# One core, conditioned transformer and state-space layers: three kinds of PSUM evacuation moved from ACT to DVE

## What is computed

```
mod = silu(cond) @ Wada + bada;  shift, scale, gate for attention and for the MLP
x = x + gate_a * attention(norm(x) * (1 + scale_a) + shift_a)
x = x + gate_m * (gelu(xm @ W1 + b1) @ W2 + b2)
```

```
h = norm(x) * (1 + scale) + shift
for each direction:  xs, z = split(h @ in_w);  xs = silu(xs);  dt = softplus(...)
    u = dt * xs;  B, C = rows of xs @ xproj            # 512 channels, 64 states
    hst[t] = hst[t-1] * exp(dt * A) + u * B;  y[t] = sum over states of hst * C
    out = ((y + xs * D) * silu(z)) @ out_w             # g is the gated output
x = x + gate * (forward + backward);  x = x + gate * ((silu(h @ w1) * (h @ w2)) @ w3)
```

## Time and profile before

| what | us |
|---|---|
| three runs | 3542.23, 3541.03, 3540.88 |
| median | 3541.03 |
| the profiled execution | 3532.22 |
| its span, first to last instruction | 3530.3 |
| mean granted TensorE clock of the profile | 0.953 |

### The profile page before, as it was taken

The page is one execution under the profiler, slowest core; times in us unless marked ns, Lnnn a source line. Parts: engine busy times, 40 slices in busy tenths (PEclk is TensorE's granted clock), DMA queues, the critical chain, the costliest instruction groups (busy, mean ns, idle before and its releaser), DMA issues.

```text
span 3530.3 us, 70435 instructions
## 1 busy us (share of the span) xinstructions
PE 3064.4 (87%) x21944; PEld 2666.9 (76%) x21944; DVE 2872.2 (81%) x3122; ACT 3086.7 (87%) x6820; POOL 2941.0 (83%) x1551
## 2 busy tenths in 40 slices
PE   6878898898988999888998889889898899988776
PEld 4567787787877877787787778778777788877765
DVE  1249998799888998789888898889988898889885
ACT  1269999999899998899998999999998999999995
POOL 0049988899888998889888898889988899899995
PEclk9589999999999999999999999999999999999999
DMA  5011111111111111111111111111111111111211
GB/s 167 0 30 45 46 42 40 48 50 45 39 48 40 52 43 40 47 47 46 43 41 46 47 46 40 48 40 51 45 41 46 45 46 44 42 43 43 54 47 27
DMA packets 170750, 162.54 MB, mean 46 GB/s; under 512 B 25834, under 2 KB 165098, under 8 KB 170356
## 3 DMA queue, kind: packets, MB, share of 16 engines
q1 hardware_dynamic: 170356, 157.69, 16.3%
HBM read 154.44 MB, written 3.18 MB: 45 GB/s over the span
## 4 chain that ended last, share of the span: by engine, by line
PE 31%; POOL 23%; issue 20%; ACT 16%; DVE 7%; SPq 1%; POOLq 0%; DMA 0%; ACTq 0%; DVEq 0%
POOL hst L395 18%; PE ps L1175 8%; PE ps L1191 7%; ACT dA L574 7%; POOL uBT L404 6%; PE ps L944 5%; ACT uBT L560 4%; DVE hst L864 3%; PE ps L953 2%; PE ps L1013 2%; PE ps L1064 1%; PE ps L991 1%; PE ps L1000 1%; PE ps L1074 1%; SPq L301 1%
## 5 line engine op out<-in xcount | busy, mean ns | idle before, releaser
L395 POOL TENSOR_TENSOR hst<-hst,C_sb 128x1024 f32<-128x1024 f32 x1024 | 2427.1, 2385 | 324.4 <-DVE hst L864 317.5
L864 DVE TENSOR_TENSOR_SCAN hst<-dA,ps 128x512 f32<-128x512 f32 x2048 | 2383.8, 1203 | 258.7 <-ACT dA L574 135.8
L574 ACT ACTIVATE dA<-dt,A 128x255 f32<-128x255 f32 x4096 | 1779.6, 500 | 102.1 <-DVE hst L864 96.8
L1175 PE MATMUL ps<-ident,uBT 128*128 128x128 f32 x8192 | 1275.3, 280 | 153.8 <-DVE hst L864 116.5
L1191 PE MATMUL ps<-ident,hst 128*128 128x128 f32 x8192 | 1273.2, 279 | 141.8 <-POOL hst L395 139.3
L1175 PEld LDWEIGHTS ps<-ident,uBT 128*128 128x128 f32 x8192 | 993.1, 145 | 286.3 <-DVE hst L864 151.0
L1191 PEld LDWEIGHTS ps<-ident,hst 128*128 128x128 f32 x8192 | 971.2, 143 | 204.0 <-POOL hst L395 203.1
L560 ACT ACTIVATE uBT<-uT,BT 128x512 f32<-128x512 f32 x1536 | 1045.6, 714 | 32.6 <-PE ps L1175 31.6
L404 POOL TENSOR_TENSOR uBT<-uT,BT 128x512 f32<-128x512 f32 x512 | 551.7, 1078 | 227.0 <-ACT uT L517 220.1
L475 ACT ACTIVATE probs<-ps,nmax 128x128 f32<-128x128 f32 (+1 forms) x256 | 104.8, 418 | 73.6 <-DVE nmax L735 73.6
L1013 PE MATMUL ps<-qk 32*128 32x256 f32 (+1 forms) x512 | 163.0, 400 | 0.6 <-DVE v L711 0.6
(11 more groups left out here) (141 smaller groups left out, 2138.3 us busy)
## 6 DMA issues: line engine op xcount, KB each, us to landing
C_sb<-c_dram SPq DMA_DIRECT2D x1024, 128.0 KB, 2.9
gate_l<-gate_rows_dram SPq DMA_DIRECT2D x16, 256.0 KB, 3.9
x_att<-in_x_dram SPq DMA_DIRECT2D x8, 256.0 KB, 3.6
w<-in_L_cond_W_dram SPq DMA_DIRECT2D x2, 1024.0 KB
out_dram<-x_glu SPq DMA_DIRECT2D x8, 256.0 KB, 3.2
hst<-in_L_cond_Wada_dram SPq DMA_DIRECT2D x1, 1536.0 KB
wg<-in_L_cond_mlp_w_dram SPq DMA_DIRECT2D x3, 512.0 KB
w_xp<-_L_cond_fwd_xproj_w_dram SPq DMA_DIRECT2D x1, 1280.0 KB
```

The costliest lines, as they stand in the source:

```text
L395: pool.tensor_tensor(h, h, C_sb[:, n % FED:n % FED + 1, :].to_broadcast([P, KI, NB]), ALU.mult).then_inc(hC_ready.sem, 1)
L574: done = act.activation(dA[:, n % NT, c, lo:hi], dt[:, d, c, lo:hi], ACT.Exp, scale=A[:, d, c, n:n + 1])
L864: dve.tensor_tensor_scan(pair(hst[:, n % NR]), pair(dA[:, n % NT]), ps[:, BANK_U + (2 * n + e) % (2 * NT), :][:, way], 0.0, ALU.mult, ALU. ...
L1175: last = pe.transpose(ps[:, BANK_U + (2 * n + e) % (2 * NT), o:o + P], uBT[:, n % NF, j, c * P:(c + 1) * P], ident[:, :])
```

## The change

Three steps change their engine, and their place among the steps does not. The `uT` copy and the `gT` copy become `tensor_copy` on DVE, of the same 128x1024 out of two PSUM banks. The scaled and shifted rows become `tensor_scalar` on DVE with the scale and shift columns as two per-partition operands, 128x256 twice for each norm. The waits for PE and the semaphores that tell of the results go with them. Each norm on DVE gets one more `sem_inc` on a counter that nobody waits for. Line numbers behind the edits shift: L864 is L865 in the new kernel, L804 is L798, L764 is L758, L782 is L776, L682 and L687 are L667 and L672.

```diff
--- before.py
+++ after.py
@@ -244,7 +244,7 @@
         pads_zero, pool_step, consts_ready, silu_ready, A_ready, mods_mm = map(
             sem, ("pads_zero", "pool_step", "consts_ready", "silu_ready", "A_ready", "mods_mm"))
         dve_setup, rows_ready, mods_ready, bn_turns = map(sem, ("dve_setup", "rows_ready", "mods_ready", "bn_turns"))
-        offset_turns, pool_turns = sem("offset_turns"), sem("pool_turns")
+        offset_turns, hT_turns = sem("offset_turns"), sem("hT_turns")
         gate0_in, gate1_in = flow("gate0_in", 16), flow("gate1_in", 16)
 
         norm_step = [flow(f"norm_step{s}", 2) for s in range(4)]
@@ -432,7 +432,7 @@
             act.wait_ge(mods_ready, 1)
             act.wait_ge(consts_ready, 7)
 
-            def norm(b, s, dst):
+            def norm(b, s):
                 for i in range(STEPS["norm"]):
                     if i == 2:
                         act.wait_ge(norm_step[s].sem, norm_step[s].at(b, 2))
@@ -452,13 +452,6 @@
                         for j in range(TT):
                             last = act.activation(xn[:, j, :], x_of[:, j, :], ACT.Identity, bias=offset[:, j:j + 1], scale=rstd[:, j:j + 1])
                         last.then_inc(xn_ready[s].sem, 1)
-                    if i == 5:
-                        act.wait_ge(xnT_mm[s].sem, xnT_mm[s].at(b, 1))
-                        for c in range(KD):
-                            col = bass.ds(b, 1)
-                            last = act.activation(dst[:, c, :], ps[:, BANK_P, c * NB:(c + 1) * NB], ACT.Identity,
-                                                  bias=mod_shift[:, s, c, col], scale=mod_scale[:, s, c, col])
-                        last.then_inc(hT_ready[s].sem, 1)
                     yield
 
             def heads(b, ti):
@@ -512,18 +505,10 @@
                     if i == 17:
                         act.wait_ge(one_ready.sem, one_ready.at(p, 1))
                         act.activation(dt[:, d], channels(uT[:, d]), ACT.Ln).then_inc(log_ready.sem, 1)
-                    if i == 22:
-                        act.wait_ge(uT_mm.sem, uT_mm.at(p, 1))
-                        act.activation(uT[:, d], ps[:, BANK_P:BANK_P + 2, :].rearrange("p a n -> p (a n)"), ACT.Copy).then_inc(uT_ready.sem, 1)
                     yield
 
             def post(p):
-                for i in range(STEPS["post"]):
-                    if i == 1:
-                        act.wait_ge(gT_mm.sem, gT_mm.at(p, 1))
-                        act.activation(gT[:, :, :].rearrange("p k n -> p (k n)"), ps[:, BANK_P:BANK_P + 2, :].rearrange("p a n -> p (a n)"),
-                                       ACT.Copy).then_inc(gT_ready.sem, 1)
-                    yield
+                yield from idle(STEPS["post"])
 
             def glu(b):
                 for i in range(STEPS["glu"]):
@@ -534,18 +519,18 @@
                     yield
 
             def layer0(b):
-                yield from norm(b, LN_ATT, hT)
+                yield from norm(b, LN_ATT)
                 yield from idle(STEPS["qkv"])
                 yield from heads(b, 0)
                 yield from heads(b, 1)
                 yield from idle(STEPS["proj"])
-                yield from norm(b, LN_MLP, hT)
+                yield from norm(b, LN_MLP)
                 yield from up(b)
                 yield from idle(STEPS["down"])
-                yield from norm(b, LN_SSM, hT_ssm)
+                yield from norm(b, LN_SSM)
 
             def close(b):
-                yield from norm(b, LN_GLU, hT)
+                yield from norm(b, LN_GLU)
                 yield from glu(b)
 
             def forcing(p, d, n):
@@ -686,6 +671,15 @@
                         for j in range(TT):
                             last = dve.bn_aggr(mv[:, j, :], stats[:, j, :])
                         last.then_inc(norm_step[s].sem, 1)
+                    if i == 5:
+                        dst = hT_ssm if s == LN_SSM else hT
+                        dve.wait_ge(xnT_mm[s].sem, xnT_mm[s].at(b, 1))
+                        dve.sem_inc(hT_turns)
+                        for c in range(KD):
+                            col = bass.ds(b, 1)
+                            last = dve.tensor_scalar(dst[:, c, :], ps[:, BANK_P, c * NB:(c + 1) * NB], mod_scale[:, s, c, col],
+                                                     mod_shift[:, s, c, col], ALU.mult, ALU.add)
+                        last.then_inc(hT_ready[s].sem, 1)
                     yield
 
             def residual(b, bank, rnd, gates, which, gate_in, mm, mul, done, x_old, x_new):
@@ -802,10 +796,17 @@
                         dve.wait_ge(dt_ready.sem, dt_ready.at(p, 1))
                         dve.wait_ge(in_ready.sem, in_ready.at(p, 1))
                         dve.tensor_tensor(pre, dt[:, d], xsT[:, :, :], ALU.mult).then_inc(u_ready.sem, 1)
+                    if i == 22:
+                        dve.wait_ge(uT_mm.sem, uT_mm.at(p, 1))
+                        dve.tensor_copy(uT[:, d], ps[:, BANK_P:BANK_P + 2, :].rearrange("p a n -> p (a n)")).then_inc(uT_ready.sem, 1)
                     yield
 
             def post(b, d):
                 for i in range(STEPS["post"]):
+                    if i == 1:
+                        dve.wait_ge(gT_mm.sem, gT_mm.at(2 * b + d, 1))
+                        dve.tensor_copy(gT[:, :, :].rearrange("p k n -> p (k n)"),
+                                        ps[:, BANK_P:BANK_P + 2, :].rearrange("p a n -> p (a n)")).then_inc(gT_ready.sem, 1)
                     if i == 8:
                         if d == 0:
                             dve.wait_ge(out_done.sem, out_done.at(b, 0))
```

## The result

Five timed runs of the changed kernel took 3517.93 to 3531.06 us, median **3522.52 us**, beside 3541.03 for the kernel before: ratio 0.995, 95% interval 0.9935 to 0.9966. It is faster by 18.5 us, where 9.8 were forecast; the time lies inside the range, the forecast ratio of 0.9972 outside the interval. The profiled execution took 3522.32 us (span 3520.5), where the sum gave 3522.4 for it.

A forecast was written before the change was run, and what follows sets the result against it. No engine was the bound throughout; PE, POOL, ACT and DVE took turns. Seven times the per-block terms gave -10.5 us, plus 0.3 and 0.4 made -9.8, taking 3541.0 to 3531 us; the 8-in-10 range was 3511 to 3558.

The forecast's parts named there:

- the one loss: GLU norm and u in the forward pass, where DVE has no gap: +2.3 us, 7 times.
- Term 1: GLU norm and u in the forward pass: DVE's added work delays PE and the GLU copies, +2.3 us, 7 times.
- Term 2: MLP norm: PE's wait before its first product goes, so it starts earlier; -1.3 us, 7 times.
- a dear case: GLU norm and u, forward pass: PE's longer stand also lowers its granted clock, costing some 4 us.
- Term 3: Attention norm: the product that waited 1.29 us starts earlier; -1.1 us, 7 times.
- Term 4: Gated output in the forward pass: ACT's decays and SiLU table load come earlier; -1.1 us, 7 times.
- Term 5: State-space norm: part of PE's 0.64 us wait goes; -0.4 us, 7 times.
- Term 6: Places near nothing: backward gated output 0, backward u +0.1 7 times, first forward pass +0.3, prologue and tail 2 x 0.2.
- A: Rival, slower: DVE's full stretch is paid and the leads elsewhere are lost; +17.5 us, 3558 us, chance 0.21.
- B: Rival, no change: leads half lost, -14, GLU and u loss stays, +16; 3540 us, chance 0.28.
- C: Rival, faster by more: the GLU norm and u loss is covered, 0 there; sum -26, 3515 us, chance 0.08.
- D: Rival: DVE becomes the bound everywhere and all 73 us show; 3614 us, chance 0.02.

The follow-up runs named there:

- att_mlp_gf: Kernel before with the attention and MLP norms' rows and the forward pass's gated-output copy moved to DVE; median 3512.71 us beside 3539.91, ratio 0.9916.
- no_u_glu: Kernel before with the attention, MLP and state-space norms' rows and both gated-output copies moved to DVE; median 3514.54 us beside 3541.29, ratio 0.9924.
- glu_u: Kernel before with the GLU norm's rows and the copy of u moved to DVE; median 3540.90 us beside 3536.78, ratio 1.0010.
- g_only: Kernel before with only the gated-output copy moved to DVE, in both passes; median 3533.96 us beside 3541.29, ratio 0.9973.
- att_mlp_g: Kernel before with the attention and MLP norms' rows and the backward pass's gated-output copy moved to DVE; median 3531.66 us beside 3536.78, ratio 0.9976.
- u_only: Kernel before with only the copy of u moved to DVE, in both passes; median 3555.24 us beside 3541.29, ratio 1.0038.

## Why the prediction was right, and where it was not

- **The sign and the mechanism** were right: DVE's extra 73 us (70 us busy in the moved rows; DVE's total rose by 57) did not show as such, and neither did ACT's 68 us of relief (its total fell by 49). The places decide, with both signs, and the one loss was named.
- **Term 1, +2.3, measured +1.8.** The step that failed is "the load waits for the fourth copy". The load came behind ACT's decays; only the SiLU behind it waits for the copy. In the kernel before decays and copy ended at the same 1552.57, so its timeline could be read either way. The DVE side was late as forecast (+2.28 to the first copy), and 1.1 us came back because the load moved under the copies. Its first distance was forecast as 15.4 us from the product to the load; it measured 14.3. Then 0.55 us are lost again between load and residual, which I had not looked at. I had also treated the two moved pieces as one sum, which happens to be right only because they are moved together: apart they cost more.
- **Term 2, -1.3, measured -1.65 in the first pair of profiles and about -2.3 against the second.** The wait gave 1.1, not 1.3: the product starts 2.00 us behind the transposes, where 1.8 was taken. The rest is PE's clock, and with both signs: in blocks 0 and 5 the kernel before had its first product at full speed and the changed kernel at the low level, and nothing was won there. I had seen the low clock in the GLU stretch and named it as a dear case there, and had not asked the same of the MLP norm, where the 2.07 us of the product in the earlier trace rows stood before me.
- **Term 3, -1.1, measured -0.7.** From the transposes to the product PE won 0.8. DVE's first copies, which were to come 0.2 earlier behind the statistics, came 0.26 later, and 0.93 were won behind them.
- **Term 4, -1.1, measured -1.2.** Right, step by step: two scans, the copy, and the load 3.28 us behind the copy's start.
- **Term 5, -0.4, measured +0.2.** DVE stood 0.78 us before the pair, so it was free in time, and still PE's product starts 7.57 us behind the statistics, before 7.39; nothing was won, and att_mlp_gf without it is as fast. The step that failed is "here ACT had fewer decays queued ahead": it had none, ACT stood 0.36 us before it made the rows, so there was no queue to save.
- **Term 6** held: backward gated output 0, backward u 0 but for the clock (+0.1 was taken), first forward pass +0.3. The tail cost about 1 us more than the 0.4 allowed.
- **From the profile to the median.** "The forecast for the median is 3541.0 - 9.8" carried the 8.8 us, by which the median lay above the profiled execution, over to the changed kernel. There the profiled execution and the median agree to 0.2 us. The profiled execution of the kernel before was a lucky one: it had the low clock behind the MLP norm in 4 blocks, the second one in 6, which is 4.9 us that the change mostly removes and the sum did not contain. If the timed runs are like the second one, that is 4.9 of the miss of 8.7 (18.5 against 9.8); it is an inference from two profiles. The other 3.8 us are not settled.
- **The rivals.** A (slower) falls: its mechanism, the full stretch of DVE, is real and cost 10.7 us in the loop, but the leads of terms 2 to 4 were not lost in POOL. B (no change) had the leads half lost: the MLP norm, the attention norm and the gated output gave 23.9 us in the loop, where their three terms come to 23.4 for as many blocks. C (term 1 covered) falls too, though the time came out a little over half way to it: the first GLU copy was 2.28 us late, which C excluded. D would have made the kernel 73 us slower. The rule of the Trainium skill (Perfetto Trace Analysis, Optimizing Scalar/DVE Operations) that it may make sense to offload work from a saturated DVE to Scalar agrees with the one place where DVE was full: leaving u and the GLU norm with ACT is worth some 8 us (no_u_glu against the change). The copies took 1.20 and 1.21 us beside a busy POOL. The Trainium skill (SBUF — State Buffer, Who interferes with whom) has it that VectorE work with at most one SBUF input, outside the 2-port modes, does not contend with GpSimd; the rows agree.

## What to carry to other kernels

Move an operation between engines place by place, not kind by kind: of the same kind of norm, one instance won 1.7 to 2.3 us a block (the MLP norm) and another alone lost 2.2 (the GLU norm), and the best kernel here moves 40 instructions where the change moves 96. Two moves that meet in one stretch have to be tried together and apart, since together they can cost less than their sum. And a time that was won by a shorter stand of PE should be read with the clock of the matmuls behind it.

## What was not expected of the hardware

At the MLP norm of the kernel before, the same schedule (transposes 5.45 us behind the statistics after a wait of 2.0 us, the first product 3.11 us behind them) was followed by a product at nearly twice its duration (2.07 for 1.13 us, granted clock 0.51 of full speed, the lower of the two levels) in 10 of 14 blocks, and by one at full speed in the other 4. PE's second wait was 1.0 to 1.4 us in the ten and 1.58 in the four, so it is not the longer idle time that goes with the low level: in the ten the matmuls between the two waits ran long already. With the rows on DVE (second wait 0.5 us or less) the second product took its 1.03 us in 48 of 49. At the products behind the attention's output (8.59 us from the scaled output, `o_sb`, to the residual instead of 6.96) and behind the residual in the forward pass (7.37 instead of 5.79) the same jump came and went between executions of one kernel and between kernels, with no edit near it. At the first place the two profiles of the kernel before have it in 1 block of 7 each, those of the changed kernel in 1 and 2, glu_u in none, g_only and att_mlp_g in 5 and u_only in 6. So one step of 1.6 us there can't be put down to an edit; whether an edit elsewhere makes the jump more frequent is not shown, since most kernels have one profile. Two profiles of one kernel differed by 6.6 us (the kernel before) and 5.8 us (the changed one).
